# Moving five steps of the second tile's iteration in a hand-ordered Macaron layer

## The reference

```python
def ffn(x):                       # k0, k1, k2 are boolean, weights are +1 or -1
    h = jnp.concatenate([x, -x], axis=-1)
    h = s0 * (h @ sign(k0));  h = relu(h) * 2      # 128*2 -> 512
    h = s1 * (h @ sign(k1));  h = relu(h) * 2      # 512 -> 512
    return s2 * (h @ sign(k2))                     # 512 -> 128

def attn(x):
    Q, K, V = (heads(x @ W.T + b) for W, b in ((Wq, bq), (Wk, bk), (Wv, bv)))
    a = softmax(einsum('bhqd,bhkd->bhqk', Q, K) / sqrt(8))
    ctx = merge(einsum('bhqk,bhkd->bhqd', a, V))
    return layernorm(ctx + x) * gamma + beta

x = x + 0.5 * ffn(layernorm(x))
x = x + attn(layernorm(x))
x = x + 0.5 * ffn(layernorm(x))
```

## Time and profile before

| | |
|---|---|
| median of 3 runs | 704.90 us |
| the three runs | 703.69, 704.90, 704.94 us |
| profiled execution | 703.69 us, of which the span is 701.6 us |
| PE busy | 659.6 us (94%) |
| DVE busy | 617.9 us (88%) |
| ACT busy | 474.4 us (68%) |
| POOL busy | 474.8 us (68%) |
| granted TensorE clock, mean | 0.998 |
| largest wait of PE in all | 16.5 us in 38 pieces, score matmuls (L1004) for row_max |

### The profile page before, as it was taken

The page is one execution under the profiler, slowest core; times in us unless marked ns, Lnnn a source line. Parts: engine busy times, 40 slices in busy tenths (PEclk is TensorE's granted clock), DMA queues, the critical chain, the costliest instruction groups (busy, mean ns, idle before and its releaser), DMA issues. The chain is left out here.

```text
span 701.6 us, 18134 instructions
## 1 busy us (share of the span) xinstructions
PE 659.6 (94%) x7042; PEld 305.8 (44%) x7042; DVE 617.9 (88%) x1229; ACT 474.4 (68%) x641; POOL 474.8 (68%) x790
## 2 busy tenths in 40 slices
PE   7888989999999999999999999999999998888887
PEld 3434333444444344444444444444434444343446
DVE  6778988999899999899899999989999998887766
ACT  3436767777777767777677777777776776766743
POOL 5556569687877868697787868787786875254330
PEclk9999999999999999999999999999999999999999
DMA  3032222232212223222322322221222221020000
GB/s 86 31 65 65 67 63 55 77 65 57 78 35 78 61 70 70 73 56 54 82 47 62 71 77 66 57 74 37 78 60 72 55 73 40 22 65 10 21 1 31
DMA packets 90964, 40.49 MB, mean 58 GB/s; under 512 B 65793, under 2 KB 90881, under 8 KB 90881
## 3 DMA queue, kind: packets, MB, share of 16 engines
q1 hardware_dynamic: 89264, 38.63, 22.2%
q10 hardware_dynamic: 1616, 0.72, 0.4%
HBM read 5.05 MB, written 4.19 MB: 13 GB/s over the span
## 5 line engine op out<-in xcount | busy, mean ns | idle before, releaser
L1325 ACT ACTIVATE probs<-ps_t,score_scale 128x1024 f32<-128x1024 f32 x252 | 280.3, 1112 | 106.7 <-PE ps_t L1017 103.9
L1671 DVE TENSOR_REDUCE row_max<-ps_s 128x4 f32<-128x1024 f32 x256 | 311.1, 1215 | 18.1 <-PE ps_s L1004 17.5
L1543 DVE SCALAR_TENSOR_TENSOR ffn_lo<-ps_z,ffn_hi 128x512 f16<-128x512 f32 x232 | 157.9, 685 | 35.1 <-ACT ffn_hi L1283 31.5
L879 PE MATMUL ps_z<-ffn_hi,w 128*128 128x512 f16 x464 | 177.1, 382 | 0.6 <-DVE ffn_lo L1543 0.4
L880 PE MATMUL ps_z<-ffn_lo,w 128*128 128x512 f16 x464 | 175.9, 379 | 0.0
L1283 ACT ACTIVATE ffn_hi<-ps_z 128x512 f16<-128x512 f32 x232 | 137.7, 594 | 41.2 <-PE ps_z L869 19.0
L1056 PE MATMUL ps_c<-probs,v_cols 128*32 128x256 f32 x2048 | 132.1, 386 | 1.5 <-ACT ctx_t L1335 1.5
L1004 PE MATMUL ps_s<-k_rows,q_rows 32*128 32x256 f16 x1024 | 100.3, 273 | 22.9 <-DVE row_max L1671 16.5
L1017 PE MATMUL ps_t<-q_rows,k_rows 32*128 32x256 f16 x992 | 97.1, 273 | 0.0
L1004 PEld LDWEIGHTS ps_s<-k_rows,q_rows 32*128 32x128 f16 x1024 | 29.0, 92 | 121.4 <-DVE row_max L1671 87.2
L1056 PEld LDWEIGHTS ps_c<-probs,v_cols 128*32 128x32 f32 x2048 | 56.8, 109 | 55.6 <-issue 27.9
(11 more groups left out here) (222 smaller groups left out, 1029.5 us busy)
## 6 DMA issues: line engine op xcount, KB each, us to landing
x<-L_attn_x SPq DMA_DIRECT2D x16, 256.0 KB, 3.0
q_rows<-q_hi SPq DMA_DIRECT2D x32, 128.0 KB, 2.1
k_rows<-k_hi SPq DMA_DIRECT2D x31, 128.0 KB, 2.1
y<-x SPq DMA_DIRECT2D x15, 256.0 KB, 2.2
q_rows<-no_max SPq DMA_DIRECT2D x16, 128.0 KB, 2.1
q_rows<-q_lo SPq DMA_DIRECT2D x16, 128.0 KB, 2.1
k_rows<-k_lo SPq DMA_DIRECT2D x15, 128.0 KB, 2.1
max_cols<-max_wide SPq DMA_TRANSPOSE x63, 2.3
```

What stands on the lines that cost most here:

```text
L879: pe.matmul(o[:], w, ffn_hi[:, 1 + k, :], start=(k == 0), stop=False)
L1325: a_.activation(probs[n % PROBS][:, j:j + 2, :], o[:], ACT.Exp, scale=score_scale[:, 0:1]).then_inc(s_exp, 1)
L1543: v.scalar_tensor_tensor(out=ffn_lo[:, use, :], in0=z_bank(f, use)[:], scalar=0.0, in1=ffn_hi[:, use, :], op0=ALU.max, op1=ALU.subtract).t ...
L1671: v.tensor_reduce(row_max[hb % 2][:].rearrange("p (a l) e -> p l a e", a=2)[:, j:j + 2, :, g % 2], ps_s[:].rearrange("p l (a k) -> p l a k ...
```

## The change

All five edits touch iteration 1 alone. The FFN pieces 5, 6 and 7 move from steps 9, 10 and 12 to steps 8, 9 and 10, and piece 9 from step 19 to 21. Contexts 6 and 7 move from steps 20 and 21 to 19 and 20, and V from step 30 to 27. The last two ffn_bn move from step 17 to 20, ffn_mv from step 18 to 22, and the first tail_bn from step 18 to 20. On GpSimd, ffn_rows_start no longer has a place of its own in iteration 1 behind split_max of step 8 to 14's maxima; it takes the place that it has in the loop, after tail_norm and the next split_max. SyncE's order stays as it is.

```diff
--- before.py
+++ after.py
@@ -43,18 +43,18 @@
 
 PIECES = 16
 PACE_ZERO = {6 + piece * 21 // 15: piece for piece in range(PIECES)}
-PACE_ONE = {1: 1, 3: 2, 5: 3, 7: 4, 9: 5, 10: 6, 12: 7, 17: 8, 19: 9, 23: 10, 24: 11, 25: 12, 26: 14, 28: 15}
+PACE_ONE = {1: 1, 3: 2, 5: 3, 7: 4, 8: 5, 9: 6, 10: 7, 17: 8, 21: 9, 23: 10, 24: 11, 25: 12, 26: 14, 28: 15}
 PACE_ALONE = {4 + piece * 27 // 15: piece for piece in range(PIECES)}
 
 
 
 AT = {"Q": 11, "K": 13, "CT0": 14, "CT1": 22, "V": 29}
-AT_ONE = {"Q": 11, "K": 13, "CT0": 15, "CT1": 22, "V": 30}
+AT_ONE = {"Q": 11, "K": 13, "CT0": 15, "CT1": 22, "V": 27}
 AT_ALONE = {"Q": 8, "K": 12, "CT0": 14, "CT1": 22, "V": 28}
 AT_ZERO = {"Q": 20, "K": 22, "V": 25}
 AT_OWN_LAST = {"CT0": 7, "CT1": 19}
 AT_CONTEXT = {0: (0, 1), 3: (2,), 4: (3,), 16: (4, 5), 19: (6,), 20: (7,)}
-AT_CONTEXT_ONE = {0: (0,), 2: (1,), 4: (2,), 6: (3,), 16: (4,), 18: (5,), 20: (6,), 21: (7,)}
+AT_CONTEXT_ONE = {0: (0,), 2: (1,), 4: (2,), 6: (3,), 16: (4,), 18: (5,), 19: (6,), 20: (7,)}
 AT_CONTEXT_EARLY = {0: (0, 1), 3: (2,), 5: (3,), 7: (4,), 8: (5,), 13: (6,), 16: (7,)}
 AT_CONTEXT_OWN = (21, 25, 29)
 PREP_USES = ("Q", "K", "V")
@@ -73,12 +73,12 @@
 AT_STATS_B_ZERO, AT_STATS_PREP_ZERO = ((17, 17, 19, 19), 20), ((28, 28, 30, 30), 31)
 AT_STATS_NEXT_ZERO = ((7,) * TT, 8)
 AT_NORM_A_ALONE = 3
-AT_STATS_B_ONE, AT_STATS_PREP_ONE = ((15, 15, 17, 17), 18), ((30, 30, 31, 31), None)
+AT_STATS_B_ONE, AT_STATS_PREP_ONE = ((15, 15, 20, 20), 22), ((30, 30, 31, 31), None)
 HEAD_PIECES = 10
 AT_STATS_SOLO = (27, 28)
 AT_STATS_TAIL, AT_STATS_TAIL_ALONE, AT_STATS_TAIL_EARLY = (16, 26), (18, 26), (11, 22)
 AT_STATS_TAIL_BEFORE = (16, 26)
-AT_STATS_TAIL_ONE = (18, 26)
+AT_STATS_TAIL_ONE = (20, 26)
 
 
 FIRST_IN_STEP = (0, 3)
@@ -810,8 +810,6 @@
                     tail_y(t - 1, 0, 1 - par, it.misc["CT0"])
                 if not it.own_contexts:
                     split_max(t, 1)
-                if it.first and it.prev:
-                    ffn_rows_start(it.next_b, x0[1 - par])
                 if it.prev:
                     tail_norm(t - 1, 0, 1 - par)
                 if it.last_full:
@@ -823,7 +821,7 @@
                     split_max(t, 1)
                 else:
                     split_max(t, 2)
-                if next_rows and it.prev and not it.first:
+                if next_rows and it.prev:
                     ffn_rows_start(it.next_b, x0[1 - par])
                 if it.prev:
                     tail_y(t - 1, 1, 1 - par, it.misc["CT1"])
```

## The result

The changed kernel takes 707.72 us in the median of 9 runs (705.72 to 710.33), the kernel before 703.69 us of 9 (702.01 to 704.94). The ratio is 1.0054 with a 95% interval of 1.0040 to 1.0068: slower by 3.8 us. The forecast was 707.6 us within 705.2 to 709.6, slower, on a median of 704.90 that later runs of before lowered to 703.7 and then 703.4. The forecast of the time is off by 0.1 us, that of the difference by 1.1 us: forecast +2.7, measured +3.8.

The account below looks back on a forecast made before the run. TensorE paces the loop from iteration 2, so iteration 2's start counts. GpSimd's lateness 2.3, transposed rows 0.3 and handover rounding 0.1 sum to +2.7 us, 707.6 us on the median of 704.90; range 705.2 to 709.6.

Parts of the forecast that it names:

- part 3: Iteration 1, statistics and GpSimd's order: GpSimd begins 3.7 us later, VectorE waits for att_y at step 26; +2.3 us.
- the clock: Rival: TensorE's idleness before step 30 lowers its clock, slowing both contexts of step 0 by 1.7 us; +4.4, 709.3; chance 0.13.
- What bounds the kernel: TensorE paces the loop from iteration 2, busy 20.16 of 20.30 us; what counts is when iteration 2 can start.
- Part 1, the pieces: FFN pieces 5 to 7 earlier: TensorE waits for VectorE's low part before piece 6; +0.7 us at step 16, bounds 0.2 and 1.0.
- Part 2, context 6: Context 6 at step 19: TensorE waits 0.7 us for the ps_c copy, covered before step 24, but delays step 20's row maximum.
- The low bound of 0.9: Row maximum of step 28 starts only 0.9 us later if earlier waits are swallowed; rival total +1.0, 705.9; chance 0.20.
- Part 4, V: V's 0.9 us of matmuls moved from step 30 to 27: gains nothing and costs nothing.
- Part 5, the transposed rows: Next FFN's transposed rows land at 111.7, after iteration 2's first FFN matmul is ready at 111.4; +0.3 us, bounds 0 and 1.8.
- GpSimd's lag of 3.7 us: Rival: iteration 2 does not absorb it, attention transposes or second FFN's rows come 1.5 us late; +4.2, 709.1; chance 0.13.
- the gaps did not fill: Rival that they fill: moved work takes TensorE's idle pieces of iteration 1; faster by 1.7 us, 703.2; chance 0.12.

Follow-up runs that it names:

- e1: Kernel before with only FFN pieces 5, 6 and 7 moved to steps 8, 9 and 10; 702.98 us in one run, 703.38 for before beside it.
- e2: Kernel before with only contexts 6 and 7 at steps 19 and 20 and piece 9 at step 21; 702.33 us in one run.
- e4: Changed kernel with pieces 5, 6, 7 and V put back to their old steps; 707.14 us in one run.
- e3: Kernel before with only the statistics' steps and GpSimd's order of the change; 704.56 us in one run.
- e10: Kernel before with three additional GpSimd tensor_tensor operations in iteration 1, writing a tile nobody reads; 707.64 us in one run.
- e5: Changed kernel with the first tail_bn back at step 18 instead of 20; 704.37 us (10 runs), ratio 1.0010 to before.
- e8: Changed kernel with V back at step 30; 707.37 us in one run.
- e7: Changed kernel with 8 filler matmuls on TensorE behind piece 15 at step 28; 706.21 us (7 runs), ratio 1.0039 to before.
- e6: Changed kernel with the second tail_bn at step 28 instead of 26, behind that step's row maximum; 704.95 us in one run.
- e11: Kernel before with 4 late fillers on TensorE, and in iteration 1 the small maxima copy ahead of Q's four copies; 702.52 us, ratio 0.9986.

## Why the prediction was right

The path that it names held in its main term, part 3, and the direction and the range held. That the time was met within 0.1 us is luck: the base of 704.90 was 1.2 us above the 703.69 of nine runs, and the clock, which the sum left out, made up for nearly as much.

**What bounds the kernel** held. A lag once made in iteration 1 stayed for twelve iterations, 3.77 to 3.74 us.

**Part 1, the pieces**, was put at +0.7 at step 16 with TensorE's wait of 0.5. Measured 0.40 us of wait, 0.77 us at the row maximum of step 16 after the head's 0.16, and 0.78 alone (e1).

**Part 2, context 6**, was put at 0.7 us, covered by the wait for the maxima, and at work only through the row maximum of step 20. Measured 0.73 us of wait, 0.01 us alone (e2), and 0.8 us on GpSimd's start once the statistics stand behind it (e4 against e3).

**Part 3, GpSimd**, was the main term: start at 97.9, att_y at 105.4, row maximum of step 28 at 106.1, +2.3. Measured 98.07, 105.5, 106.27, and +2.37 for iteration 2. VectorE's stop was 1.46 us, just under the 1.5 to 2 that it named. e10 gives the mechanism by itself and e5 removes it with one number. The low bound of 0.9 for the case without parts 1 and 2 was not tested cleanly, since e3 had a late copy.

**Part 4, V**, was put at zero: e8 gives 2.35 against 2.37.

**Part 5, the transposed rows**, was put at +0.3 behind the late iteration. In the changed kernel it was hidden by the slow contexts; with the clock kept up (e7) it shows as 0.35 us of wait. e6 shows that it would have cost the whole 2.7 without VectorE's stop.

**Where a size was off** is the sum: +2.7 forecast, +3.8 measured. The term that was missing from the sum is the one that stood among the rivals with a chance of 0.13, the clock. The forecast gave it 1.7 us, for both contexts wholly in a slow stretch. It measured 0.9 us in the loop (e7). The slow stretch ended at about 112.1 us, ahead of the end of the second context, so the two took 3.00 us against 1.93 in e7, 1.1 more and not 1.7; they also began 0.2 us later behind slow scores, and 0.35 us would have been spent waiting for the transposed rows anyway. It was priced from the right rows but left out of the sum, although the prediction itself named 2.2 us of idleness and the stretch of the earlier trace rows came after a wait of only 1.11 us:

```profile
594.31 0.94 PE L858 MATMUL ps_z<-ident,ffn_xn 128*128 128x128 f32 x4 [1.11 <-DVE ffn_xn L1583]
```
The Trainium skill, "TensorE: Matmul & The Clock Gate", section "What's actually happening", says that the clock is halved after idleness; the runs now agree at this place (0.50 from 109.9 to 112.1 us behind waits of 2.00 and 1.44 us). Which waits bring a fall is not settled: e6 waited 1.86 us without one. What remains of the 3.8, about 0.2 us, is within the interval of the ratio.

The other rivals fell. GpSimd's lag of 3.7 us was absorbed in iteration 2 (at row maximum 40 and after, no further loss), and the gaps did not fill.

## What to carry to other kernels

An engine that is idle a third of the time can set the pace if one in-order neighbour waits for its result: when GpSimd's queue is reordered, ask when its first item becomes ready, since the whole packed chain moves by that. Edits that each measure as nothing or little can cost together when one is hidden by slack that the other uses up, so each combination needs its own chain of starts. And a new wait on TensorE of two microseconds can cost twice, once for itself and once for the slower clock behind it, so price both; fillers show which part is which.

## What the runs showed of the hardware

The clock fell to its 1.2 GHz level in the same stages in some executions and not in others, with the same waits in front (1.11 and 1.12 us before the transposes of iteration 14; the granted clock behind them was 0.58 from 594 to 597 us before, and the changed kernel's contexts there took 1.07 us, the time at full clock). The spans of one kernel lie in groups by their mean clock, so the falls go with most of the spread between runs here; one in iteration 14 costs 1.4 us. The changed kernel's wait of 2.0 us, with 8 fillers put into it, left the clock at 1.00 (e7), while 0.9 us of useful matmuls behind a wait of 2.38 us did not keep it up (e8). A wait of 1.86 us without fillers left it at 1.00 as well (e6), so these runs do not show which length of wait brings a fall.

The 128 KB copies of Q between on-chip tiles landed in 2.1 us in every profiled execution but for one of them in e3, which took 3.1 us, and the step that waited for the small copy behind it came 0.93 us late there. The same copies of K took 2.1 to 2.7 us. SyncE needs about 0.6 us to issue each such copy. Behind four of them the small copy was issued 3.83 us after its transpose (93.12 and 96.95 us, before), ahead of them 2.39 us after it (97.37 and 99.76 us, e11), and 0.86 us of that gain reached the loop.
